# Two normalized convolutions on one core: from 32x32 products to mostly 32x64 products, with output rows dealt out in fours

## What is computed

```python
x = x + conv3x3(_gn(x), L0_weight * mask)      # padding 1, mask from |weight| and a threshold
x = x + conv5x5(_gn(x), L1_kernel) + bias      # padding 2; the reference goes by way of an FFT

def _gn(v, G=16, eps=1e-05):
    g = v.reshape(B_, G, C_ // G, H_, W_)
    m = jnp.mean(g, axis=(2, 3, 4), keepdims=True)
    s = jnp.var(g, axis=(2, 3, 4), keepdims=True)
    return ((g - m) / jnp.sqrt(s + eps)).reshape(v.shape)
```

## Time and profile before

| | us |
|---|---|
| median of 3 runs | 855.02 (852.67 to 856.11) |
| profiled execution, its own time | 854.08 |
| its span | 852.3 |
| TensorE busy | 780.7 (92%) |
| VectorE busy | 692.6 (81%) |
| ScalarE busy | 319.7 (38%) |
| GpSimd busy | 322.4 (38%) |

### The profile page before, as it was taken

How to read it: one execution, slowest core, us unless ns; L and a number is a source line. 1 busy time by engine, 2 the same in 40 slices (tenths; PEclk the granted TensorE clock), 3 DMA queues, 4 the chain that set the end, 5 groups by cost and what they waited for, 6 DMA issues and landing times.

```text
span 852.3 us, 108960 instructions
## 1 busy us (share of the span) xinstructions
PE 780.7 (92%) x52277; PEld 694.1 (81%) x52277; DVE 692.6 (81%) x1008; ACT 319.7 (38%) x408; POOL 322.4 (38%) x164
## 2 busy tenths in 40 slices
PE   0874689999999999999999999999999999998995
PEld 0553579888989889889988989988998989987884
DVE  6877599899897989799898989899897968675432
ACT  0312134443443434443443434444343434443221
POOL 1035043333434443233444444333344444333331
PEclk9997799999999999999999999999999999999998
DMA  8999638788695968788685978878695737563413
GB/s 179 222 219 234 149 83 212 197 207 206 178 223 139 224 171 212 193 211 203 173 220 139 225 180 212 198 198 212 171 228 139 205 95 189 121 167 80 103 49 99
DMA packets 83778, 150.51 MB, mean 177 GB/s; under 512 B 21152, under 2 KB 28576, under 8 KB 79648
## 3 DMA queue, kind: packets, MB, share of 16 engines
q1 hardware_dynamic: 78624, 144.88, 69.0%
q10 hardware_dynamic: 4608, 4.23, 2.2%
q0 software_dynamic: 512, 1.05, 0.5%
HBM read 75.60 MB, written 33.59 MB: 128 GB/s over the span
## 4 chain that ended last, share of the span: by engine, by line
PE 78%; DVE 11%; issue 4%; DMA 3%; SPq 2%; DVEq 1%; ACT 1%; ACTq 0%; POOLq 0%; POOL 0%
PE psum L790 78%; DVE x L620 3%; SPq L242 2%; DMA mid_bands<-mid 1%; DMA x_bands<-x_dram 1%; DVE x_bands L605 1%; DVE bn_in L543 1%; DVEq L643 1%; DVE bn_out L648 1%; DVE mid_bands L605 1%; DVE mid L640 1%; DVE product L575 0%; DVE x_lo L628 0%; DVE deviation L579 0%; DVE gscale L594 0%
## 5 line engine op out<-in xcount | busy, mean ns | idle before, releaser
L354 POOL TENSOR_TENSOR mid<-mid,conv_out 128x512 f32<-128x512 f32 x122 | 300.4, 2492 | 471.9 <-ACT conv_out L387 471.9
L790 PE MATMUL psum<-x_hi,s 32*32 32x512 f16 x25600 | 373.1, 378 | 17.8 <-issue 10.3
L790 PEld LDWEIGHTS psum<-x_hi,s 32*32 32x32 f16 x25600 | 339.7, 88 | 42.1 <-issue 17.2
L790 PE MATMUL psum<-x,s 32*32 32x512 f16 x13824 | 225.3, 386 | 19.4 <-DVEq L643 12.0
L790 PEld LDWEIGHTS psum<-x,s 32*32 32x32 f16 x13824 | 174.8, 88 | 70.1 <-issue 40.1
L790 PE MATMUL psum<-x_lo,s_hi 32*32 32x512 f16 x12800 | 186.4, 376 | 3.2 <-issue 3.2
L790 PEld LDWEIGHTS psum<-x_lo,s_hi 32*32 32x32 f16 x12800 | 176.4, 88 | 8.3 <-issue 5.0
L628 DVE TENSOR_TENSOR x_lo<-mid_bands,x_hi 128x2560 f16<-128x2560 f32 x32 | 103.9, 3247 | 33.6 <-PE psum L790 31.6
L620 DVE TENSOR_TENSOR x<-x_bands,x 128x2304 f16<-128x2304 f32 x32 | 101.3, 3166 | 36.3 <-PE psum L790 36.3
L387 ACT ACTIVATE conv_out<-psum,bias,unscale 128x512 f32<-128x512 f32 x122 | 90.4, 769 | 61.1 <-PE psum L790 58.3
L396 ACT ACTIVATE s<-s_lo 128x800 f16<-128x800 f16 x29 | 25.3, 871 | 158.1 <-PE psum L790 158.1
(11 more groups left out here) (80 smaller groups left out, 196.5 us busy)
## 6 DMA issues: line engine op xcount, KB each, us to landing
x_own<-x_dram SPq DMA_DIRECT2D x128, 256.0 KB
mid_bands<-mid SPq DMA_DIRECT2D x496, 64.0 KB
out_dram<-mid SPq DMA_DIRECT2D x116, 256.0 KB
x_bands<-x_dram SPq DMA_DIRECT2D x96, 288.0 KB
x_bands<-x_dram SPq DMA_DIRECT2D x32, 272.0 KB
mid_bands<-mid SPq DMA_DIRECT2D x224, 32.0 KB
every_mv<-mv_scratch ACTq DMA_DIRECT2D x16, 256.0 KB, 3.7
out_dram<-mid SPq DMA_DIRECT2D x24, 128.0 KB
```

Of the source, the lines that this page charges most:

```text
L354: nc.gpsimd.tensor_tensor(m, m, conv_out[:, b, :], ALU.add).then_inc(out_added, 1)
L790: ins = nc.tensor.matmul(psum[quad(j), bank + i, :].rearrange("p (a w) -> p a w", a=A), w[quad(i), at, :], src[quad(i), A * j + dy:A * (j ...
```

## The change

In words:

- **Rows.** A half is now 64 rows in one piece (`band`, `own_rows`), and within a band of 16 rows column j of the array takes rows j, j + 4, j + 8 and j + 12. Loads of `x_own`, stores and moves of `mid` therefore go row by row (`as_rows`, `piece`). The rows next to a band of the same half travel with the 16 moves of the half; for the edges between the two halves of an image two moves of one row each are left in either direction.
- **Products.** Output rows 2J and 2J + 1 read one input row with two neighbouring vertical taps. `pairs` issues these as products of 32x64 (two taps' weights side by side, 64 PSUM partitions), `singles` the remaining tap of each column as 32x32. The vertical taps of the weights are stored in reverse order for that. A full step has 624 products of 32x64 and 384 of 32x32.
- **TensorE's code.** High and low weights and images have buffers of their own, nothing is rewritten between visits, and a step is one block of straight code: 3x3 on the high image, 5x5 on the high image, 3x3 on the low image, 5x5 on the low image. Within them the order of `pairs` and `singles` is pairs, pairs, singles, singles; singles, singles, pairs, pairs; pairs, singles; singles, pairs. The three last steps have a block of their own with a second copy of the 5x5 code. Before the first full step TensorE waits for all the 5x5 weights.
- **Other engines.** ScalarE no longer copies weights; it normalizes `mid` and the bands of the halves 1 to 3, with a bias that VectorE prepares (`nbias`), and clears their padding. VectorE normalizes the other bands. Its eviction of 3x3 moves behind the group statistics and the statistics of x. SP's order at the start is changed: some band loads go behind the moves of the first halves.

The core of the diff:

```diff
         def own_rows(image, r, j):
-            return image.rearrange("c (i r j a) w -> r j c i (a w)", i=BANKS, r=2, j=Q)[r, j]
+            return image.rearrange("c (r i m j) w -> r j c (i m) w", r=2, i=BANKS, j=Q)[r, j]
...
+        def piece(h, i, j):
+            first = A * i - (1 if j >= 2 and i else 0)
+            last = A * (i + 1) + (1 if j < 2 and i + 1 < BANKS else 0)
+            top = 2 + j + A * (first - A * i)
+            return (mid_bands[quad(i), h % MB_SLOTS, top:top + A * (last - first - 1) + 1:A, :],
+                    as_rows(mid, j, h % MID_SLOTS)[:, first:last, :])
...
-            load_own(0)
             load_own(1)
             load_bands(4)
-            load_bands(5)
-            sp.wait_ge(norm1, 2)
-            load_bands(6)
             move_mid(0)
             load_own(2)
+            load_bands(5)
             move_edges(0, 1, 0)
             load_own(3)
+            move_edges(0, 0, 1)
+            load_bands(6)
             load_bands(7)
-            move_edges(0, 0, 1)
...
+            def scale_by(which, v):
+                ...
+                nc.scalar.activation(v, v, ACT.Identity, bias=nbias[:, at], scale=gscale[:, at]).then_inc(act_scaled, 1)
+                act.wait_ge(act_scaled, by_scalar)
...
             for s in range(STEPS + 1):
                 gathered = exchanged(s - 1)
                 if has5(s - 1):
+                    k = s - 1 - LAG
+                    for b in range(BANKS if k < LATE else HALF_BANKS):
+                        take_conv5(k, b)
...
+                    if has5(s + 1):
+                        normalize5(s + 1 - LAG)
+                    if has3(s + 1):
+                        high3(s + 1)
+                    if has5(s + 1):
+                        high5(s + 1 - LAG)
                 if len(gathered) > 1:
                     take_root(gathered[1])
                 if exchanged(s) and s >= LAG:
                     spread_stats(s)
...
+            def pairs(w, src, k, bank, start=False, every=None):
+                for dx in range(k):
+                    x0 = 2 - k // 2 + dx
+                    for dy in range(1, k):
+                        at = dx * k + k - 1 - dy
+                        for i in range(Q):
+                            for J in range(2):
+                                top = 2 * J + dy
+                                ins = nc.tensor.matmul(
+                                    psum[2 * C * J:2 * C * (J + 1), bank + i, :].rearrange("p (a w) -> p a w", a=A),
+                                    w[quad(i), at:at + 2, :].rearrange("p t o -> p (t o)"),
+                                    src[quad(i), top:top + A * (A - 1) + 1:A, x0:x0 + W],
+                                    start=start and dx == 0 and dy == 1, stop=True, skip_group_check=True,
+                                    tile_position=(i * C, 2 * C * J))
...
+            with nc.body("whole_step", valid_engines=only):
+                hint = pe.mark_branch_hint_location()
+                high_image3()
+                high_image5()
+                low_image3()
+                low_image5(step)
+                pe.br_lt(step, HALVES, on_true="whole_step", on_false="before_last").branch_hint(hint)
...
+            with nc.body("last_steps", valid_engines=only):
+                high_image5()
+                low_image5(step)
+                pe.br_lt(step, STEPS, on_true="last_steps", on_false="all_done")
```

More of the change, by code:

```diff
@@ L345, in _ @@
                 for j in range(Q):
-                    pool.dma_start(mid_bands[quad(i), 1, 2 + A * j:2 + A * (j + 1), :],
-                                   mid[quad(j), 1, i, :].rearrange("p (a w) -> p a w", a=A),
-                                   ).then_inc(mid1_moved, 16)
+                    to, rows = piece(1, i, j)
+                    pool.dma_start(to, rows).then_inc(mid1_moved, 16)
             def add_out(k, b):
@@ new lines, in singles @@
+            def singles(w, src, k, bank, start=False):
+                for dx in range(k):
+                    x0 = 2 - k // 2 + dx
+                    for i in range(Q):
+                        for j in range(Q):
+                            dy = 0 if j % 2 == 0 else k - 1
+                            at = dx * k + k - 1 - dy
+                            ins = nc.tensor.matmul(
+                                psum[quad(j), bank + i, :].rearrange("p (a w) -> p a w", a=A), w[quad(i), at, :],
+                                src[quad(i), j + dy:j + dy + A * (A - 1) + 1:A, x0:x0 + W],
+                                start=start and dx == 0, stop=True, skip_group_check=True, tile_position=(i * C, j * C))
+                return ins
@@ new lines, in high_image5, with low_image5 @@
+            def high_image5():
+                pe.wait_ge(x5_hi_go, 1)
+                singles(s5_hi, x5_hi, K5, X5_BANK, start=True)
+                singles(s5_lo, x5_hi, K5, X5_BANK)
+                pairs(s5_hi, x5_hi, K5, X5_BANK, every=x5_hi_go)
+                pairs(s5_lo, x5_hi, K5, X5_BANK).then_inc(a5_whole, 1)
+            def low_image5(step):
+                pe.wait_ge(x5_lo_go, 1)
+                singles(s5_hi, x5_lo, K5, X5_BANK).then_inc(b5_begun, 1)
+                pe.reg_add(step, step, 1)
+                pairs(s5_hi, x5_lo, K5, X5_BANK, every=x5_lo_go).then_inc(b5_whole, 1)
@@ L922, in _ @@
[L922 to L927 removed]
             nc.switch_bb("lead_end")
+            pe.wait_ge(w5_split, 3)
             pe.addr_align(256, offset=0, max_nops=0)
[L931 to L932 removed]
+            pe.br("whole_step")
```

434 lines of the change are left out of this document (156 added, 278 removed).

## The result

The changed kernel takes 900.78 us (median; 899.52 to 901.56) where the kernel before took 854.75 in the same series: a ratio of 1.054, 95% interval 1.051 to 1.056. It is slower by 46 us; I had predicted 843.5, with a range to 886. The profiled execution took 901.0 us, its span 899.2.

The account below looks back on a forecast made before the run. TensorE, busy 92% and streaming, was taken as the bound. Lead 106.6, body 659.1 and tail 75.1 made a span of 840.8 us; with 1.8 around it and 0.9 for the median, 843.5 us, range 820 to 886.

Parts of the forecast that it names:

- The step that failed: VectorE's even step: the 3x3 eviction ends at 19.9 us, TensorE wants bank 3 at 23.3; hidden, slack 3.4 us.
- The products and seams: TensorE's full step: 102 rounds, 22.13 us, plus seams of 0.42, 0.36 and 0.40: 23.31 us.
- Rival 1: TensorE: changes between tiles drain the array, 0.43 us each; step 24.64 us, total 884 us, slower; chance 0.14.
- The 6.4 us of irregular stalls, kept: Body: 6.4 us of irregular stalls beyond the 28 steps of the kernel before, added unchanged to reach 659.1 us.
- The clock: Body: granted clock 1.00, the higher level of 2.4 GHz, taken as no issue; no time charged.
- Rival 3: Late 3x3 end makes VectorE and ScalarE late: 0.5 us a step, 857 us, no change; chance 0.13.
- ScalarE: break-even, charged at nothing: Top of a step: ScalarE's eviction of four banks before 5x5 may start just about fits; nothing charged, range widened.
- DMA: Body: 512-byte pieces at 37 ns make 20.2 us of queue time a step, under 23.3; hidden, but close.
- Rival 2: DMA: 512-byte pieces bind; at 50 ns a step is 25.6 us, total 908 us; chance 0.13.
- Lead: Before the body: 5x5 weights ready at 62.8 us let step 3 start earlier; gain 9 us (0 to 14), lead 106.6.
- Tail: Three 5x5-only steps and last stores: 68.1 plus 7.0, including 8 us of code loads (0 to 15): 75.1 us.
- Rival 5: TensorE's loop outgrows the instruction store: a reload of 1.4 us or more a step, 883 us and up; chance 0.05.

Follow-up runs that it names:

- more_changes: w5_early with the 5x5 high image's stages as pairs, singles, pairs, singles, so 8 tile changes a step instead of 4: 859.43 us, ratio 1.001 to the kernel before.
- scale_late: The changed kernel with VectorE's second scale in even steps behind the 3x3 eviction instead of ahead of it: 842.37 us, ratio 0.985 to the kernel before.
- root_early: The changed kernel, VectorE's list untouched, with ScalarE's second root moved ahead of the two high images: 844.54 us, ratio 0.985 to the kernel before.
- long_pieces: w5_early with x_own loads and output stores in pieces of 2048 bytes instead of 512 (output rows misplaced): 844.68 us, ratio 0.984 to the kernel before.
- w5_early: scale_late with VectorE taking up the 5x5 weights' bound ahead of the first 3x3 eviction: 840.94 us, ratio 0.982 to the kernel before.
- tail_shared: w5_early with the last three steps running the loop's 5x5 code through branches instead of a copy: 837.3 us, ratio 0.9745 to the kernel before.
- all_small: w5_early with every tap as 32x32 products in the same straight code, about 3264 TensorE instructions a step: 1752.17 us (one run).
- before_late_eviction: The kernel before with VectorE's 3x3 eviction behind the second group statistics, the statistics of x and the second scale: 874.48 us (one run).
- tail_no_hint: tail_shared without the branch hint at the head of the loop, nothing else changed: 1230.14 us (one run).

## Why the prediction was wrong

The step that failed is the slack of 3.4 us that I gave VectorE's eviction of 3x3: in every second step it was 2.8 us late. By the stretches of the sum (840.8 predicted, 899.2 measured, 58.4 apart) the body is 47.1 us too long, the lead 10.6 and the tail 0.7:

- **The products and seams: right.** 102 rounds a step in 1008 products; a stage of 160 pairs is busy 4.61 us, less the last product's 0.38, which is 4.23 for 19.9 rounds of 8, 0.213 each. The undisturbed step is 23.17 against 23.31, closer than its parts: 102 rounds of 0.213 are 21.7 instead of 22.1, and the seams are 1.4 instead of 1.2. The gaps at a change are 0.30 and within a tile 0.08 to 0.20; more_changes gives 0.14 to 0.17 us for a change, where I had 0.10. Rival 1 (0.43) is refuted.
- **The 6.4 us of irregular stalls, kept: wrong, to my gain.** 28 x 23.17 is 648.8, and without the pauses and the falls of the clock the body has only 0.2 more.
- **VectorE: the step that failed.** "... it ends at 0.4 + 21.6 - 2.4 + 0.3 of waits = 19.9 us, and gives bank 3 back, which TensorE wants at 23.3. Hidden, slack 3.4 (it was over 5)." The work was right (20.45 us busy in the step of 26.14), the slack was not: I summed VectorE's own instructions and charged 0.3 us for all waits, without following the root, the operand in that list that ScalarE makes. The root stands on ScalarE behind `high3`, which waits for `c3_whole`, the semaphore that tells that 3x3 is complete. I had the end of 3x3 (17.8 us into a step; measured 235.37 - 217.62 = 17.75) in hand, and the trace of before has the rest: 17.8 + 0.1, 2.1 and 2.3 for the two images, so 22.3 for the root, 1.2 for root and scale, 2.5 for the eviction, 26.0 in all, against 23.3. That is 2.7 late; the pause measured is 2.78 us and the step 26.14. Eviction first on VectorE hides it entirely (scale_late), the root first on ScalarE as well (root_early).
- **The clock: not thought of.** "The clock is no issue in the body" held for the kernel before. A wait of 2.8 us cost 3.0, and 1.66 more in 11 of 13 cases. Together 57.3 us in the body, less the 10.3 that the step and the dropped stalls gave: the 47.1 by which the body is too long.
- **Rival 3** had the place (VectorE late because 3x3 ends late) with 0.5 us a step and 13%. The mechanism was its, the size was 2.0 us a step: it was priced from slacks and not from the order of the lists.
- **ScalarE: break-even, charged at nothing: right for what it looked at,** the drain that lets 5x5 begin: in the body of scale_late TensorE waits for another engine once, 0.4 us for that drain. The same list holds the root of the step that failed, and that paragraph does not follow it.
- **DMA: right in the body.** The share is 0.84 from 180 to 750 us of scale_late (my 20.2 of 23.3 is 0.87), a piece costs about 36 ns by long_pieces, and TensorE has no wait for a DMA there. Rival 2 is refuted. In the lead of w5_early ScalarE does wait for a move.
- **Lead: 117.2 instead of 106.6.** VectorE took up the weights' bound only at 61.50, behind the statistics of the second 3x3 output; GpSimd began at 64.38 and not at 55.5. That is step 3 at 70.1 instead of 63. The other 3.5 us are in step 3, whose waits for code are 17.0 us in sum where before had 13.1. Taking the bound up earlier starts step 3 at 63.57 in w5_early, as I had it, but at 66 to 70 in three other kernels with that order, and the body starts at 112.5 to 118.3, not at 106.6. Of the gain of 9 at most 3 were there: I named one next bound and not what stands behind it, the 5x5 image and the code.
- **Tail: 75.8 instead of 75.1.** The copy's code loads cost 3.5 us (8 charged, 0 to 15 allowed), by the first tail step of w5_early and tail_shared; in after that step is 1.7 us longer still, at a lower granted clock. The rest I did not take apart, so that the tail comes out is in part luck.
- **Rival 5** (the loop outgrows the store) did not happen at 2026 instructions, and does for all_small's loop of some 3280 (no run lies between), at another price than my "1.4 us or more": 900 / (27680 / 1632) = 53 us a step, 30 us more, since all blocks are loaded again and not one. Losing the hint does the same to the loop that fits, at 37.8 us a step.
- **That scale_late meets the sum is luck.** Its span is 839.4 us against 840.8, but its lead is 9.5 us longer (116.1), its body 9.4 shorter (649.7) and its tail 1.6 shorter (73.5) than summed.

## What to carry to other kernels

When a step's list on one engine is reordered, walk each operand that comes from another engine back through that engine's list until you reach the bottleneck engine, and add the times on that path; the sum of an engine's own work says nothing of the order. An item that gives a buffer back to the bottleneck goes ahead of every item that waits for someone else. Where straight code just fills the instruction store, its length and the hint on its back branch are part of the design: look at the packets of the instruction queue in each profile.

## What I had not expected of the hardware

- A wait of TensorE of 2.8 us was followed by 3.4 us at a granted clock of 0.50 in 11 of 13 cases, and one of 1.45 to 1.48 us (before_late_eviction) in none of 13.
- Straight code that isn't loaded comes at one block of 16 KB in 3.4 to 3.5 us at best (336.32 to 339.71 in tail_no_hint, 706.53 to 710.02 in all_small), and in 37.8 / 9 = 4.2 us on average in tail_no_hint. 128 products of 32x64 run in 16 rounds, 3.4 us, so code once through is nearly bound by it; 128 of 32x32 run in 8, 1.7 us, and are bound by it. The Trainium skill (Runtime: NRT & Kernel Launch, Instruction fetch mechanics) calls the crossing of a block mostly hidden. The loops that stay loaded agree with its 2048 instructions for TensorE (2026 stay, some 3280 don't); its "mostly hidden" does not hold here.
- The hint on a back branch: 837 us with it, 1230 without.
- GpSimd's additions of 128x512 took 1.81 us on average in after and 2.33 in scale_late, with the same operands. The trace shows beside what they are slow. In after's step from 217.62 the first two run while VectorE makes its low images (217.95 to 224.34) and take 2.52 and 3.60 us, the other two 1.28 each; the next four run beside VectorE's eviction and statistics and take 1.24 each:

```profile
219.35 8.69 POOL L360 TENSOR_TENSOR mid<-mid,conv_out 128x512 f32<-128x512 f32 x4 [23.33 <-ACT conv_out L424]
241.91 4.97 POOL L360 TENSOR_TENSOR mid<-mid,conv_out 128x512 f32<-128x512 f32 x4 [13.87 <-ACT conv_out L424]
```

In scale_late the eviction no longer comes late, and the groups of four in the body take 8.6 to 10 us (that from 326.58 runs beside the low images of 328.24 to 335.33). No run changes this overlap alone.
